# Attention values as stationary plain-fp32 operands, sums over keys on GpSimd, norms applied to projected rows

## The reference, cut to what matters

```
q = (x @ Wq) as 16 heads of 128;  k, v = x @ Wk, x @ Wv as 8 heads, each serving 2 q heads
log_g = log_sigmoid(6.906768 + x @ Wg);  logG = cumsum(log_g over time)
a[t, s]  = (q_t . k_s / sqrt(128))**2 * exp(logG_t - logG_s)     for s <= t, else 0
y_t      = sum_s a[t, s] v_s / (sum_s a[t, s] + 1e-6)
out      = y @ Wc + bc
```

## Time and profile before

| | us |
|---|---|
| median of 3 runs | 2798.73 (2795.59 to 2799.43) |
| profiled execution | 2799.59 |
| its span, first to last instruction | 2797.8 |
| attention, about | from 50 to 1880 of the span |

### The profile page before, as it was taken

The page is one execution under the profiler, slowest core; times in us unless marked ns, Lnnn a source line. Parts: engine busy times, 40 slices in busy tenths (PEclk is TensorE's granted clock), DMA queues, the critical chain, the costliest instruction groups (busy, mean ns, idle before and its releaser), DMA issues.

```text
span 2797.8 us, 42331 instructions
## 1 busy us (share of the span) xinstructions
PE 2360.3 (84%) x14564; PEld 2064.3 (74%) x14568; DVE 1966.2 (70%) x3734; ACT 1648.0 (59%) x3246; POOL 892.8 (32%) x622
## 2 busy tenths in 40 slices
PE   5988987999999799899899999977979999999210
PEld 4877886888788688788788888976868877777110
DVE  3767777788998687998778889876756666665114
ACT  3655665576666576666566666752357777776110
POOL 2010002000181100145111007200658888787202
PEclk8998998999999899999999999987989999999555
DMA  4665563011131102022101103014579999998215
GB/s 138 215 195 177 171 224 118 22 54 35 38 127 35 42 22 76 23 78 91 50 22 53 35 28 124 33 64 144 194 211 219 227 211 216 215 223 165 49 40 184
DMA packets 221345, 320.71 MB, mean 115 GB/s; under 512 B 15616, under 2 KB 191488, under 8 KB 221088
## 3 DMA queue, kind: packets, MB, share of 16 engines
q1 hardware_dynamic: 173712, 250.63, 28.0%
q0 software_dynamic: 47232, 66.48, 12.4%
q10 hardware_dynamic: 144, 0.39, 0.0%
HBM read 160.42 MB, written 157.02 MB: 113 GB/s over the span
## 4 chain that ended last, share of the span: by engine, by line
PE 48%; DVE 19%; DMA 12%; issue 7%; SPq 6%; ACT 4%; POOL 4%; DVEq 0%; PEldq 0%; POOLq 0%; ACTq 0%
PE bank L569 29%; PE bank L900 8%; SPq L680 5%; DVE a_lo L1373 4%; DMA y_part<-y_e,xr 4%; PE bank L579 4%; DMA xr<-slots 3%; PE bank L902 3%; DMA decay_all<-decay_dram 2%; DVE sums L1383 2%; PE bank L998 2%; POOL slots L1715 2%; POOL y_part L1726 1%; DVE a L1367 1%; PE bank L914 1%
## 5 line engine op out<-in xcount | busy, mean ns | idle before, releaser
L900 PE MATMUL bank<-v_pair,a_hi 128*128 128x258 f32 x2304 | 592.4, 326 | 52.8 <-DVE sums L1383 48.8
L1726 POOL DMA_INDIRECT y_part<-y_e,xr x264 | 453.2, 1717 | 224.7 <-ACT y_e L1232 104.9
L1373 DVE TENSOR_TENSOR a_lo<-a,a_hi 128x512 fp32r<-128x512 f32 (+1 forms) x640 | 452.6, 707 | 99.1 <-ACT a_hi L1130 98.3
L902 PE MATMUL bank<-v_pair,a_lo 128*128 128x130 f32 x2304 | 521.0, 226 | 0.0
L900 PEld LDWEIGHTS bank<-v_pair,a_hi 128*128 128x128 f32 x2304 | 439.8, 191 | 97.4 <-DVE sums L1383 52.2
L902 PEld LDWEIGHTS bank<-v_pair,a_lo 128*128 128x128 f32 x2304 | 444.7, 193 | 21.7
L1130 ACT ACTIVATE a_hi<-a 128x512 fp32r<-128x512 f32 (+1 forms) x640 | 377.8, 590 | 75.6 <-DVE a L1367 71.9
L1699 POOL CAST wc_hi<-wc_raw 128x512 fp32r<-128x512 f32 x32 | 19.9, 622 | 1101.0 <-PE bank L569 613.7
L1117 ACT ACTIVATE a<-bank,c_s 128x512 f32<-128x512 f32 x384 | 263.4, 686 | 117.3 <-PE bank L569 62.1
L1715 POOL DMA_INDIRECT slots<-rows,slot_u x192 | 214.2, 1116 | 278.9 <-DVE slot_u L1541 219.8
L569 PE MATMUL bank<-q_hi,k_hi 128*128 128x512 f32 (+1 forms) x640 | 262.9, 411 | 17.4 <-ACT a L1119 17.4
(11 more groups left out here) (202 smaller groups left out, 5737.6 us busy)
## 6 DMA issues: line engine op xcount, KB each, us to landing
slots<-acc SPq DMA_DIRECT2D x64, 972.0 KB, 12.7
w_raw_f<-in_wffn SPq DMA_DIRECT2D x70, 624.0 KB, 6.7
xr<-slots SPq DMA_DIRECT2D x64, 648.0 KB, 5.1
decay_all<-decay_dram SPq DMA_DIRECT2D x128, 128.0 KB, 3.0
w_raw<-in_wall SPq DMA_DIRECT2D x31, 512.0 KB, 5.6
wc_raw<-in_wall SPq DMA_DIRECT2D x32, 256.0 KB, 5.0
y_part<-acc SPq DMA_DIRECT2D x7, 768.0 KB, 10.0
y_part<-y_e,xr POOLq DMA_INDIRECT x264, 5.2
```

The costliest lines, as they stand in the source:

```text
L900: e.matmul(bank[2 + k][:, 0:VW], a_hi[i4][:, r, cols], v_pair[i][:, s, :], start=first, stop=False, skip_group_check=True)
L902: ins = e.matmul(bank[2 + k][:, 0:VH], a_lo[i4][:, r, cols], v_pair[i][:, s, 0:VH], start=False, stop=last, skip_group_check=True)
L1373: e.tensor_tensor(a_lo[u % 4][:, :, 0:w], a32[u % 2][:, :, 0:w], f32(a_hi[u % 4][:, :, 0:w]), ALU.subtract).then_inc(s_a_lo)
L1726: e.indirect_dma_start(out=y_part[part], out_offset=bass.IndirectOffsetOnAxis(ap=xr[r][:, j, TOKEN_COL:TOKEN_COL + 1].bitcast(U32), axis=0 ...
```

## The change

- `av`: one plain fp32 product per unit, values stationary (`v`, unsplit), squares (`a32`, unsplit) moving, 512 or 256 columns. The output is born transposed (value features on the partitions), one bank per group, three banks in turn (`NJ`). Six buffers of squares (`NA`), three score banks (`NS`). `pair`, `a_hi`, `a_lo`, `v_pair`, `turn`, `merge` and `normalise` are gone.
- Decay of the off-diagonal part: `decay` multiplies the output bank in place on VectorE by `f_b`, an Exp over the 256 columns made by ScalarE in `em`.
- Diagonal units are multiplied by the square root of the decay before they are squared (VectorE reads the score bank, ScalarE squares).
- Sums over keys: GpSimd adds the squares of a group elementwise into `nacc` (and multiplies by `f_b`); `norm` on TensorE then sums over the partitions with 4 one-column fp32 products against ones per group, VectorE adds 1e-6 and takes the reciprocal.
- `yt` splits the output (ScalarE high, VectorE low); `project` runs once per query head r, and `add` multiplies the projected rows by the reciprocal norm while adding into `acc`.
- Values: computed for two heads at once (`PAIR`), with x stationary, 256 columns, so that they need no transposing. Their weights have a load and a split of their own (`wv_in`).
- The order of the units: the two diagonal units of group g stand behind the off-diagonal units of group g + 1. The places of the other tasks in the list move with it.

```diff
-UNITS = [(g, s) for g in range(NG) for s in range(2 * g + 2)]
+UNITS = []
+for g_ in range(1, NG):
+    UNITS += [(g_, s_) for s_ in range(2 * g_)] + [(g_ - 1, 2 * g_ - 2), (g_ - 1, 2 * g_ - 1)]
+UNITS += [(NG - 1, 2 * NG - 2), (NG - 1, 2 * NG - 1)]
+NA, NS, NJ = 6, 3, 3
 # schedule()
-    args_at = {2: 2, 6: 3, 9: NG, 17: NG + 1}
+    args_at = {2: 2, 8: 3, 15: NG, 17: NG + 1}
-    load_at = {7: 0, 8: 1, 10: 2, 18: 3}
-    late_by = ((3, 2), (2, 2), (2, 6), (2, 2))
+    load_at = {7: 0, 11: 1, 17: 2, 19: 3}
...
+                must_at = [i * (NU - ahead) // len(must) for i in range(len(must))]
...
-        if s >= 2 * g:
-            do("merge", n, g, s - 2 * g)
+        if s == 2 * g - 1:
+            do("decay", n, g)
         if s == 2 * g + 1:
-            do("normalise", n, g)
-            late.append((u + late_by[g][0], "turn", n, g))
+            do("yt", n, g)
+            late += [(u + 1, "norm", n, g, 0), (u + 1, "project", n, g, 0), (u + 2, "project", n, g, 1)]
...
-        elif at in background_at and background:
+        elif background:
             route_step(n // H - 1, background.pop(0))
-        if (g, s) == (1, 1):
+        if at == 5:
             if n + 1 < HEADS:
                 do("wc_in", n + 1)
             if n + 2 < HEADS:
                 do("w_in", n + 2)
+                if n % PAIR == 0:
+                    do("wv_in", n // PAIR + 1)
 # TensorE
+            def av(u):
...
+                once.wait_ge(s_sq, u + 1)
...
+                if first and j >= NJ:
+                    once.wait_ge(s_nrm, j - NJ + 1)
+                if s == 2 * g and g:
+                    once.wait_ge(s_off, f_nth(n, g))
...
+                    e.matmul(dst, v[n % 3][:, s, :], a32[u % NA][:, :, :], start=first, stop=False,
+                             skip_group_check=True).then_inc(s_av)
+            def norm(n, g):
+                j = n * NG + g
+                once.wait_ge(s_yt_lo, j + 1)
+                once.wait_ge(s_nadd, nadd_of[unit_of[n, g, 2 * g + 1]])
+                for tt in range(2):
+                    for r in range(R):
+                        k = tt * R + r
+                        ins = e.matmul(av_bank(j)[:, k:k + 1], nacc[j % NJ][:, r, tt * P:(tt + 1) * P], ones[:, 0:1], start=(k == 0),
+                                       stop=True, skip_group_check=True)
+                ins.then_inc(s_norm)
 # ScalarE, score(u)
+                if u >= NA:
+                    once.wait_ge(s_av, u - NA + 1)
+                    once.wait_ge(s_nadd, nadd_of[u - NA])
 # GpSimd
+            def add_up(out_, a, b, op=ALU.add):
+                nonlocal nadd
+                once.wait_ge(s_nadd, nadd)
+                nadd += 1
+                e.tensor_tensor(out_, a, b, op).then_inc(s_nadd)
+            def av(u):
...
+                once.wait_ge(s_sq, u + 1)
+                if s == 0:
+                    once.wait_ge(s_norm, j - NJ + 1)
...
+                elif s == 1:
+                    add_up(total[:, :, :], a32[(u - 1) % NA][:, :, :], squares[:, :, :])
+                elif s == 2 * g + 1:
+                    add_up(total[:, :, P:GROUP], total[:, :, P:GROUP], squares[:, :, 0:P])
+                elif s:
+                    add_up(total[:, :, :], total[:, :, :], squares[:, :, :])
+                if s == 2 * g - 1:
+                    once.wait_ge(s_f, f_nth(n, g))
+                    add_up(total[:, :, :], total[:, :, :], f_b[g - 1][:, :].unsqueeze(1).to_broadcast([P, R, GROUP]), ALU.mult)
```

More of the change, by code:

```diff
@@ L179, in schedule @@
     late, must, background = [], [], []
+    must_at = ()
     def run_late(u):
-        for item in sorted((x_ for x_ in late if x_[0] <= u), key=lambda x_: x_[1]):
+        for item in [x_ for x_ in late if x_[0] <= u]:
             late.remove(item)
[L184 to L187, removed]
+            _, what, n_, g_, r_ = item
+            if what == "norm":
+                do("norm", n_, g_)
             else:
-                put_off.append((on_spare("project", n_, g_), ("add", n_, g_)))
+                put_off.append((on_spare("project", n_, g_, r_), ("add", n_, g_, r_)))
     catch_up()
     for u in range(ahead):
-        if u:
-            do("pair", u - 1)
         do("score", u)
@@ L348, in build @@
     for task in order:
[L349 removed]
+        if task[0] in ("col", "val"):
             split_nth[task] = len(split_nth) + 1
[L351 to L353 removed]
+    last_qk = {n: max(spare["col", n, which, r, T // 512 - 1] for which, r in ((1, 0), (0, 0), (0, 1))) for n in range(HEADS)}
+    last_val = {p: max(spare["val", p, q] for q in range(TILES // 2)) for p in range(HEADS // PAIR)}
+    masked_nth, nadd_of, unit_of = {}, {}, {}
+    nadd = 0
     for u, (n, g, s) in enumerate(UNITS_ALL):
+        unit_of[n, g, s] = u
         if s >= 2 * g:
             masked_nth[u] = len(masked_nth) + 1
[L357 to L365, removed]
[L366 to L372 removed]
+        if s < 2 * g:
+            nadd += (s > 0) + (s == 2 * g - 1)
+            nadd_of[u] = nadd + (s == 0) - (s == 2 * g - 1)
+        else:
+            nadd += 1
+            nadd_of[u] = nadd + (g == 0 and s == 0)
     raw_at, raw_loads = {}, 0
@@ L638, in xt @@
             def xt(b, half):
-                splits, halves = before["xt", b, half]
-                once.wait_ge(s_xt_lo, halves)
-                once.wait_ge(s_w_lo, splits if splits > 1 else 0)
+                once.wait_ge(s_xt_lo, 2 * b + half)
                 t0 = b * T + half * T // 2
-                e.dma_start(xt_raw, xT[:, :, t0:t0 + T // 2]).then_inc(s_xt_in, 16)
+                e.dma_start(xt_raw[:, :, :], xT[:, :, t0:t0 + T // 2]).then_inc(s_xt_in, 16)
             def acc_in(b):
@@ L878, in av @@
                 n, g, s = UNITS_ALL[u]
-                i, i4 = n % 2, u % 4
-                halves = [1] if s == 2 * g + 1 else [0, 1]
-                t_off = P if s == 2 * g + 1 else 0
-                once.wait_ge(s_a_lo, u + 1)
-                once.wait_ge(*out_of(("val_turn", n, s // 4)))
-                for tt in halves:
-                    first = s in (0, 2 * g)
-                    last = s == 2 * g - 1 or s == 2 * g + tt
+                j = n * NG + g
+                first = s == 0
@@ L1403, in turn_lo @@
[L1403 to L1411 removed]
+                    n0, g0 = divmod((mine - 3) // 2, NG)
@@ L1675, in pool_program, with split_done @@
             once = Once(e)
+            split = 0
+            def split_done():
+                nonlocal split
+                split += 1
+                once.wait_ge(s_pool, split)
             def acc_in(b):
```

455 lines of the change are left out of this document (214 added, 241 removed).

## The result

The changed kernel took 3099.1 us (median of four runs, 3091.5 to 3107.7), the kernel before 2798.6 in the same set: 1.108 times as long, 95% interval 1.105 to 1.111. The forecast was 3056 us, the range 2925 to 3125.

A forecast was written before the change was run, and what follows sets the result against it. Attention was taken as bound by TensorE's queue, with GpSimd's in-order queue newly holding it. Heads without fills -25, fills +94.5, sends +175.5, late loads +12 gave +257 on 2799.6: forecast 3056 us, range 2925 to 3125.

The forecast's parts named there:

- TensorE's work per head: Attention heads on TensorE: +0.7 us of work, net -1.0 with waits, a quiet head going from 53.4 to 52.4 us.
- The fourth rival: Values' products on TensorE: plain fp32 would not hold the clock up, +530 us, about 3590 us; chance 0.04.
- GpSimd's new work: GpSimd in each head: 25 us of sums on top of some 6 us of weight splits, keeping up in quiet heads.
- The sends: Indirect stores in GpSimd's queue, batches 1 to 3: TensorE waits for sums behind them, 58.5 us per batch, 175.5 in all.
- The loads behind the fills: Heads 0 to 6: `wc_raw` issued behind the fills delays GpSimd's split and sums, +13.5 us a head, 94.5 in all.
- The 12 us for late loads in routing heads: One routing head in each of batches 1 to 3: sync engine reaches `wc_raw` late behind `x1t` stores, +4 each.
- the wait for the low half: `norm` on TensorE asks for the transposed output's low half: 0.2 us a group, rounded to nothing where other work lies between.
- The boundary: At a batch's end `acc_in` waits about 13 us for a load, in place of the present gate stall: no net change.
- The second: Rival: only the sends hurt, the fills' loads come in time because longer heads spread them, about 2930 us; chance 0.14.
- the third: Rival: GpSimd's sums slower beside VectorE, 2.6 us an operation, setting all heads' pace at 57 us, about 3165 us; chance 0.07.
- the first rival: TensorE need not wait for GpSimd because buffers of squares and sums absorb the delay, about 2740 us, faster; chance 0.09.

The follow-up runs named there:

- f2: Changed kernel with stores spread out, weight loads issued before the fills and `norm` one unit later, as third set's control: 2736.9 us, 0.978 of the kernel before.
- e5: Changed kernel with stores spread out, weight loads before the fills and `norm` one unit later, run in the second set: 2761.5 us, 0.948 of the kernel before.

## Why the prediction came out as it did

The total came out 43 us over the forecast and inside the range, and the sign, the two expensive places and their cause are right. But that it is so near is in part luck: one wait was left out that cost some 90 us, and two terms were too dear by some 40.

- **TensorE's work per head: near, with the wrong sign for the head.** 52.4 us was forecast for a quiet head, 52.6 measured between two splits, at a clock of 1.00. But the forecast was a difference, 1.0 us less than 53.4, and that is to be compared in one and the same place. Heads 13 and 14 have neither routing steps nor fills. They take 106.8 us before, 53.4 each, and 109.6 after: 1.4 more each, not 1.0 less. TensorE is busy for 99.4 us of them before and 98.5 after. So the work was forecast a little high (0.4 less a head, for 0.7 more), since a 512-column plain fp32 product costs 0.86 us and not 0.92, 1.1 us a head. What came on top is waits for the low half. The prediction's own sum is also off by 0.2 a head: 0.7 - 1.5 is -0.8. The fourth rival (plain fp32 doesn't hold the clock up) is out.
- **GpSimd's new work: right.** A full addition took 1306 ns, forecast 1320 from the earlier trace rows. The estimate by the Trainium skill (GPSIMD Engine Reference, Performance versus the Vector engine), 1.1 us, was further off. All of it was 699 us more; the forecast of 800 had counted the gaps between operations. TensorE's waits for the sums are 220 us, for the 270 forecast.
- **The sends: right in place and cause, too dear by a sixth.** Forecast 58.5 us per batch, 175.5 in all; spreading them gave 149.2. The head with the stores takes 98.9 us, forecast about 110. The waits came in the three pieces shown above and two more (the 8.1 for ScalarE's square, and 3.0 for VectorE's `ub`), 45 us together for the 55 forecast; the rest is slower work around them.
- **The loads behind the fills: right in cause, too dear by 13 us.** Forecast 94.5 against the kernel before; heads 0 to 6 grew by 81.1. Undoing the order gave 112.0, more than that, because the kernel before too had longer heads there (57.3), by its wait for `decay_all`. The 12 us for late loads in routing heads did not come: GpSimd does wait for `wc_raw` there (11.5 us at 703.70), but TensorE does not, and with the loads early the three batches are 1 us shorter together.
- **The step that was missed: the wait for the low half.** The prediction has it in the words "I leave 0.2 us a group, rounded down to nothing". It was 90.3 us in 74 pieces. In quiet heads it is some 0.5 us a group; in heads with routing steps up to 4.9, where the low half stands behind those steps, a table load and `em` in ScalarE's and VectorE's lists. That these engines have far less to do (48% and 39% busy) didn't help, because it is the order of one chain that counts. Without the sends the prediction's terms give a batch 4 us less than before. With the stores spread out, the three batches are 20, 32 and 26 us longer than before, so some 30 us each were missed, 90 in all. From there the later `norm` (in f2, whose early loads do nothing in these batches) takes 81 us back. The sends (some 27) and the fills (13) that were too dear hide 40 of them, and the expert stage and smaller things another 8. Moving `norm` alone by one unit gave back 119.5.
- **The boundary: nothing, as forecast,** to 3 us (heads 14 and 15 take 131.5 for 128.6).
- **The rivals.** That TensorE would not wait for GpSimd has failed by the 220 us above. The second (only the sends hurt) is out by the 112 us of the loads, the third (2.6 us an addition) by the 1306 ns. With all three edits, and no work taken away, the kernel comes to 2737 us, near the 2740 of the first rival. That the numbers meet is luck: it had 1.0 us less for every head, where the batches are as before, and 4.9 less in a fill head, where it is 6.8.

The cause of each of the three waits is shown by its own edit and by their sum. Not shown is that the value product itself gains anything over the kernel before; by the table it gains nothing outside the fill heads. Not settled either is the stall of the kernel before while its stores go out. It is profiled on the second chip alone; the 2900.6 us of the first set would fit it.

## What to carry to other kernels

Moving work to an idle engine with an in-order queue is paid by what already stands in that queue: list its long runs and its waits for loads, and ask at which of them the new consumer will arrive. Break the runs up and issue loads ahead of bulk stores before judging the move; here this turned 1.07 to 1.11 times the time into 0.95 to 0.98. Then count the gain by stretch before you credit it to the change: here it lies in the heads where the old order had a wait of its own. And a consumer that asks one unit after its producer pays for every step that the producer's engine has in between: give it a second unit, and don't round small waits to nothing when they come 128 times.

## What the runs showed of the hardware

- A plain fp32 product of 512 columns took 0.86 us, an f32r one 0.23. With the plain ones a quiet head had the full granted clock of 1.00 (2.4 GHz); with the same product in one pass the mean over attention fell from 0.95 to 0.88.
- Twelve indirect stores hold GpSimd's queue for 15.5 us (from 823.67 to 839.14 in the changed kernel), yet with all 48 spread over three heads, and the other two edits in, heads 8 to 15 take 457.3 us for the 457.6 of the kernel before.
- The fills' ten stores a head did not slow a head at all once the loads went ahead of them. Two such heads of e5, TensorE busy for 98.28 of 101 us at 237 GB/s:
```profile
169.00:270.00 101.00, 98.28 (x485) 74.41 (x484) 52.88 (x111) 42.70 (x78) 57.04 (x52) 1.00 0.74 237
```
- The same kernel differed by 4% between chips, through a stall in one place (TensorE busy for 36 of 50 us instead of 49.5, at a clock of 0.83 instead of 1.00), which another arrangement of the same work does not have.
